# One shared expert in two parts around the private experts, and the third normalisation and router table inside the block of the weighted sum

## The reference

```python
xn = _layernorm(x, axis=-1)
x = x + _L0_gnn_ref(xn, edge_index, edge_weight, ...) + _L0_mix_ref(xn[None], ...)[0]
x = x + _L0_ffn_ref(_layernorm(x, axis=-1)[None], ...)[0]
xn = _layernorm(x, axis=-1)
x = x + _L1_gnn_ref(xn, edge_index, edge_attr_2, ...) + _L1_mix_ref(xn[None], ...)[0]
x = x + _L1_ffn_ref(_layernorm(x, axis=-1)[None], ...)[0]

def _L0_ffn_ref(x, Wr, W1s, b1s, W2s, b2s, W1p, b1p, W2p, b2p):
    shared = gelu(x @ W1s + b1s) @ W2s + b2s
    rw = jax.nn.softmax(x @ Wr, axis=-1)
    topw, topi = jax.lax.top_k(rw, K)
    ...
    return shared + routed

...
h = (x_flat @ W_gat).reshape(M, HEADS, NUM_EXPERTS)
a_src = (h * att_src).sum(-1)
a_dst = (h * att_dst).sum(-1)
```

## Time and profile before

| what | us |
|---|---|
| three runs, median (lowest to highest) | 3953.55 (3953.06 to 3957.26) |
| the profiled execution | 3953.38 |
| its span, first to last instruction | 3951.6 |
| busy: PE, DVE, ACT, POOL | 2606.2, 1907.8, 988.4, 2575.3 |
| mean granted clock of PE | 0.771 |

### The profile page before, as it was taken

The page is one execution under the profiler, slowest core; times in us unless marked ns, Lnnn a source line. Parts: engine busy times, 40 slices in busy tenths (PEclk is TensorE's granted clock), DMA queues, the critical chain, the costliest instruction groups (busy, mean ns, idle before and its releaser), DMA issues. The chain is left out here.

```text
span 3951.6 us, 42737 instructions
## 1 busy us (share of the span) xinstructions
PE 2606.2 (66%) x9484; PEld 1776.0 (45%) x9485; DVE 1907.8 (48%) x4550; ACT 988.4 (25%) x3007; POOL 2575.3 (65%) x4612
## 2 busy tenths in 40 slices
PE   0560004888875989999329666662357775697998
PEld 0350001333334778888325444442222223595776
DVE  8568822555553111111136688884257775553222
ACT  0120000000001212222012266552067775202111
POOL 0888886888878887777878888888278881000000
PEclk9975555565555999999769888886589996558999
DMA  1100004333341126666232222241011110000000
GB/s 47 33 17 19 8 2 148 104 105 105 104 83 56 35 74 193 197 194 194 82 93 56 50 51 50 50 48 6 3 10 8 8 8 2 0 0 27 11 11 33
DMA packets 179887, 229.35 MB, mean 58 GB/s; under 512 B 67275, under 2 KB 144445, under 8 KB 178749
## 3 DMA queue, kind: packets, MB, share of 16 engines
q0 software_dynamic: 81792, 103.39, 12.2%
q1 hardware_dynamic: 96828, 116.40, 9.3%
q10 hardware_dynamic: 1152, 8.39, 0.5%
HBM read 192.28 MB, written 35.73 MB: 58 GB/s over the span
## 5 line engine op out<-in xcount | busy, mean ns | idle before, releaser
L375 POOL DMA_INDIRECT slots_gnn<-rec_gnn,slot_row_gnn x782 | 775.9, 992 | 275.7 <-issue 153.7
L791 PE MATMUL banks<-rows_gnn,one_hot 128*128 128x256 f32 x832 | 459.2, 665 | 252.7 <-DMA rows_gnn<-support,slot_gnn 240.7
L1520 POOL DMA_INDIRECT arena<-table,slot_gnn x440 | 466.4, 1060 | 99.1 <-issue 88.9
L766 POOL DMA_INDIRECT rows_gnn<-support,slot_gnn x416 | 393.9, 947 | 96.4 <-issue 68.8
L791 PEld LDWEIGHTS banks<-rows_gnn,one_hot 128*128 128x128 f32 x832 | 198.9, 294 | 512.4 <-DMA rows_gnn<-support,slot_gnn 466.1
L766 POOL DMA_INDIRECT rows_router<-table_g,slot_router x304 | 310.6, 1022 | 130.8 <-POOLq L764 71.7
L1891 PE MATMUL banks<-score_diags,one_hot_m 128*128 128x512 f32 x608 | 291.9, 627 | 133.0 <-DVE group_max L1917 83.8
L1605 PE MATMUL banks<-weighted,one_hot 128*128 128x260 f32 x880 | 276.4, 470 | 73.6 <-ACT weighted L1581 72.9
L375 POOL DMA_INDIRECT slots_router<-rec_router,slot_row_router x256 | 260.4, 1017 | 72.4 <-issue 45.6
L1224 PE MATMUL banks<-xT,w 128*128 x960 | 267.7, 439 | 51.5 <-DMA w<-in_w2s 26.2
L469 PE MATMUL banks<-ident,xn 128*128 128x128 f32 x200 | 50.2, 396 | 349.2 <-DVE xn L450 349.2
(11 more groups left out here) (378 smaller groups left out, 4288.0 us busy)
## 6 DMA issues: line engine op xcount, KB each, us to landing
w_private<-in_w1p SPq DMA_DIRECT2D x32, 1024.0 KB
w_private<-in_w2p SPq DMA_DIRECT2D x32, 1024.0 KB
slots_gnn<-rec_gnn,slot_row_gnn POOLq DMA_INDIRECT x782, 2.1
slot_x<-zero_rows ACTq DMA_DIRECT2D x8, 1024.0 KB, 11.5
slot_rows<-slot_x SPq DMA_DIRECT2D x32, 256.0 KB
slot_y<-slot_out SPq DMA_DIRECT2D x32, 256.0 KB
arena<-table,slot_gnn POOLq DMA_INDIRECT x440
rows_gnn<-support,slot_gnn POOLq DMA_INDIRECT x416, 2.7
```

The costliest lines, as they stand in the source:

```text
L375: pool.indirect_dma_start(e.slots, bass.IndirectOffsetOnAxis(e.rows[:, j:j + 1], 0), e.rec[:, j, :], None)\
L766: pool.indirect_dma_start(e.rows_in[:, k, :], None, table, bass.IndirectOffsetOnAxis(row, 0))\
L791: pe.matmul(c.bank[:, k // per, 0:D], hot[:, k, :], e.rows_in[:, k, :], start=k % per == 0, stop=k % per == per - 1).then_inc(used, 1)
L1520: pool.indirect_dma_start(c.raw[:, t % RAW_RING, :], None, c.table1, bass.IndirectOffsetOnAxis(row, 0))\
```

## The change

Four things. First, the shared expert's weights are kept in a buffer of the whole block and loaded at its start (`load_shared0`), and its five chunks are done in two stages: three chunks before the private experts, two after them. In the second of these DVE also adds the fetched rows (`add_fetched0`), a few before each tile's own additions, up to a goal: 12 rows before tile 0 of its first chunk, two more with each tile, then 37 before the first tile of the second chunk, and the rest behind the last. Second, normalisation 3 and `table_g_stage` become stages of the sum's block, and Block C goes. Third, since more now lives in that block's memory, `AHEAD` is 120 for 128 and the ring 216 for 224 tiles. Fourth, the router's records are cut otherwise: 58, 40 and 158 for 58, 76, 34 and 88.

```diff
-EARLY = (58, 134, 168)
+EARLY = (58, 98)
+SHARED_FIRST = 3
...
+def load_shared0(c, block, weights):
+
+    w1, w2, b1, b2, biases, loaded = weights
+
+    @block.sync
+    def _(sp):
+        sp.dma_start(w1[:, 0, :, :], c.a["w1s"].rearrange("(k p) f -> p k f", p=P)).then_inc(loaded[0], 16)
+        sp.dma_start(w2[:, 0, :, :], c.a["w2s"].rearrange("(f p) d -> p f d", p=P)).then_inc(loaded[0], 16)
...
+        else:
+            for tile in range(nt):
+                beside(dve, tile, nt, y_done, tile + CHUNK_TILES)
+                add(0, tile, c.X[:, begin * CHUNK_TILES + tile, :], 1.0, tile % CHUNK_TILES)
+            beside(dve, nt, nt, y_done, nt + CHUNK_TILES)
...
+def add_fetched0(c):
+
+    state = [0]
+
+    def upto(dve, tile, tiles, y_done, done):
+        total = T * CHOSEN
+        t = tile % CHUNK_TILES
+        per_chunk = total // (tiles // CHUNK_TILES)
+        goal = total if tile == tiles else tile // CHUNK_TILES * per_chunk + per_chunk // 2 + 2 * t
+        dve.wait_ge(y_done, done)
+        while state[0] < goal:
...
-AHEAD = 128
-RAW_RING = 224
-ARENA = 224 * 2 * MSG
+AHEAD = 120
+RAW_RING = 216
+ARENA = RAW_RING * 2 * MSG
...
-                    scatter_records(c, block, s, eg, EARLY[0], EARLY[1])
                     fetch_outputs0(c, block, s)
+                    w_shared = expert_weights(c, s, "0", 1, FF0)
+
+                    load_shared0(c, block, w_shared)
...
-                                  lambda st, m: private_experts_stage(c, block, st, m)):
+                                  lambda st, m: shared(st, m, (0, SHARED_FIRST), None),
+                                  lambda st, m: private_experts_stage(c, block, st, m),
+                                  lambda st, m: shared(st, m, (SHARED_FIRST, CHUNKS), add_fetched0(c))):
...
-                        scatter_records(c, block, s, eg, EARLY[1], EARLY[2])
+                        scatter_records(c, block, s, eg, EARLY[0], EARLY[1])
                         gather_messages(c, block, s, e1, m + 2, m + 3)
-                        scatter_records(c, block, s, eg, EARLY[2])
+                        scatter_records(c, block, s, eg, EARLY[1])
...
-                        with ExitStack() as st:
-                            sum1_stage(c, block, st, e1)
+                        for stage in (lambda st, m: sum1_stage(c, block, st, e1, m),
+                                      lambda st, m: norm_stage(c, block, st, "3", m, False),
+                                      lambda st, m: table_g_stage(c, block, st, m)):
+                            m += 1
+                            with ExitStack() as st:
+                                stage(st, m)
...
-                    with nc.Block() as block:
-                        for stage in (lambda st, m: norm_stage(c, block, st, "3", m, False),
-                                      lambda st, m: table_g_stage(c, block, st, m)):
-                            m += 1
-                            with ExitStack() as st:
-                                stage(st, m)
-                    c.clear_spent()
```

More of the change, by code:

```diff
@@ new lines, in experts_stage @@
+def experts_stage(c, block, ctx, name, met_n, F, experts, b1_rows, b2_rows, gates, weights=None,
+                  chunks=None, beside=None):
+    E, FC = len(experts), F // P
+    begin, end = (0, CHUNKS) if chunks is None else chunks
+    nc_, nt = end - begin, (end - begin) * CHUNK_TILES
+    w1, w2, b1, b2, biases, loaded = expert_weights(c, ctx, name, E, F) if weights is None else weights
+    hid = c.sb(ctx, f"hidden_{name}_{begin}", [P, FC, 2, HALF_CHUNK])
+    part = c.sb(ctx, f"expert_out_{name}_{begin}", [P, 2, D])
+    h_ready = c.sem(ctx, f"hidden_ready_{name}_{begin}")
+    h_done = c.sem(ctx, f"hidden_gelu_{name}_{begin}")
+    y_ready = c.sem(ctx, f"out_ready_{name}_{begin}")
+    y_done = c.sem(ctx, f"out_added_{name}_{begin}")
+    biased = c.sem(ctx, f"out_biased_{name}_{begin}")
@@ L1205, in _ @@
     def _(sp):
[L1206 to L1212, removed]
+        if weights is None:
+            sp.dma_start(b1[:], b1_rows).then_inc(biases, 16)
+            sp.dma_start(b2[:].rearrange("p e d -> p (e d)"), b2_rows.partition_broadcast(P)).then_inc(biases, 16)
+            for e, (W1, W2) in enumerate(experts):
+                if e >= 2:
+                    sp.wait_ge(y_ready, (e - 1) * T)
+                sp.dma_start(w1[:, e % 2, :, :], W1.rearrange("(k p) f -> p k f", p=P)).then_inc(loaded[e % 2], 16)
+                sp.dma_start(w2[:, e % 2, :, :], W2.rearrange("(f p) d -> p f d", p=P)).then_inc(loaded[e % 2], 16)
         meet(sp, met, met_n)
@@ L1254, in _, with add @@
     def _(dve):
+        def add(e, tile, x, gate, t):
+            dve.wait_ge(y_ready, tile + (e * nt + 1))
+            dve.wait_ge(y_done, tile + (e * nt + CHUNK_TILES))
+            dve.tensor_tensor(part[:, 0, :], c.bank[:, 4 + t % 4, 0:D], b2[:, e, :], ALU.add)\
+                .then_inc(biased, 1)
+            dve.wait_ge(biased, tile + (e * nt + 1))
+            dve.scalar_tensor_tensor(x, part[:, 0, :], gate, x, ALU.mult, ALU.add).then_inc(y_done, 1)
         dve.wait_ge(biases, 32)
@@ L1269, in _ @@
-        meet(dve, met, met_n)
+        if beside is None:
+            for e in range(E):
+                with dve.Fori(0, nc_) as i:
+                    for t in range(CHUNK_TILES):
+                        tile = i * CHUNK_TILES + t
+                        at = i * CHUNK_TILES + (begin * CHUNK_TILES + t)
+                        x = c.X[:, ds(at, 1), :].rearrange("p a d -> p (a d)")
+                        gate = 1.0 if gates is None else gates[:, ds(at, 1), e:e + 1].rearrange("p a b -> p (a b)")
+                        add(e, tile, x, gate, t)
+        else:
[3 more added lines that the diff above has]
+            beside(dve, nt, nt, y_done, nt + CHUNK_TILES)
@@ L1549, in sum1_stage @@
     used = c.summed1
+    met = c.met
     per = GROUP // P
@@ L1588, in _ @@
         act.activation(rise[:], rise[:], ACT.Exp).then_inc(rise_exped, 1)
+        meet(act, met, met_n)
     @block.tensor
@@ L1624, in _ @@
         mm.then_inc(units, 1)
+        meet(pe, met, met_n)
     @block.vector
@@ L1767, in _ @@
         ch.then(dve.tensor_tensor(x, x, agg[:, :, 0:FEAT], ALU.add))
+        meet(dve, met, met_n)
+    @block.sync
+    def _(sp):
+        meet(sp, met, met_n)
 NE1 = 4
@@ L2271, in build @@
                     records.close()
+                    c.table_g = nc.dram_tensor("table_g", [NP, ROW_G], F32, kind="Internal").ap()
+                    c.tab = c.sb(l1, "tab_g", [P, T, ROW_G])
+                    c.edge_tab = c.sb(l1, "edge_tab", [P, T, 2 * NE1])
+                    c.high = c.sb(l1, "high", [P, T, NE1])
+                    c.lift = c.sb(l1, "lift", [P, 1])
                     with ExitStack() as s, nc.Block() as block:
```

84 lines of the change are left out of this document (33 added, 51 removed).

## The result

The changed kernel takes 3902.26 us (median of 4 runs, 3899.91 to 3902.39) and the kernel before 3953.31 (4 runs, 3952.53 to 3957.26): a ratio of 0.9867, 95% interval 0.985 to 0.9885. The profiled execution took 3902.39 us around a span of 3900.7, 51.0 less than before. The forecast was 3896, a gain of 57.0; the measured gain is 51.0, so it was 6 us smaller than worked out.

What follows compares the result with a forecast made beforehand. POOL's queue of indirect DMAs plus the hole before the router's gather was taken as the bound up to 2871 us. Hole -57.8 and last scatter +0.8 gave -57.0: 3953.4 to 3896 us, range 3884 to 3911.

Steps and rivals of the forecast that it cites:

- POOL's queue as the bound: From 1176 to 2871 us, POOL's indirect DMAs plus the hole before the router's gather were taken to set the time.
- The sum's shape: Shorter hole before the gather, -57.8 us, plus POOL's last scatter, +0.8, giving -57.0; the first block's 96 us bring nothing.
- that sign: POOL's last scatter was to lie within 5 us of 2799.7; moving by over 10 us would refute the prediction.
- Records beside the weights: Second graph's records before the fetch: 64 more meet private weights' traffic, 1.372 us each for 1.273; net +4.2 us.
- The end of the first block: Between the first block and the next: no term of its own; the second normalisation was expected near 1918.
- The wait at tile 120: POOL's messages: with AHEAD 120, POOL waits for the mix's end at 2232.4; +5.6 us of new wait.
- 70 more scatters: Router records behind the messages at the end of POOL's queue: 70 more at 1.27 us each, +88.9 us.
- The end of the second block: Between POOL's last scatter and the slot load before the router's gather: 11.3 us, low bound 6.1, 2 allowed upward.
- PE and the second part: Last two shared-expert chunks on PE, beside the fetch, 1837 to 1906; DVE ends at 1915.2 without holding POOL back.
- The rival of the lower clock: PE's second shared part falls to 1.2 GHz behind a meeting: +79 us, 3975 us, slower; chance 0.03.
- the cover: Moved normalisation and router table were to end at 2685 us, 115 us ahead of POOL's last scatter.
- The normalisation beside POOL: Third normalisation beside POOL's scatters costs one us; by the skill's two-port rule about 9 us, giving 3905 us.

Runs made afterwards that it cites:

- One part alone: Normalisation 3 and router table moved into the sum's block, shared expert whole, against the kernel before: 3899.7 us, ratio 0.9878.
- the other alone: Shared expert split, but normalisation 3 and router table in their own block, ring 224, AHEAD 128, against the kernel before: 3954.3 us, ratio 1.0016.
- twice the stage behind POOL's back: Changed kernel with normalisation 3 done twice in the sum's block: 3902.8 us, ratio 0.9879 to the kernel before.
- the first four runs: Four variants on one chip (stages moved only, shared expert split only, normalisation 3 doubled, two shared chunks early): 3899.7, 3954.3, 3902.8, 3916.9 us; kernel before 3948.4.
- two chunks first and the old goals: Changed kernel with two shared-expert chunks before the private experts and three behind, fetched-row goals unchanged: 3916.9 us, ratio 0.9919 to the kernel before.
- nine records moved: Kernel with only the stages moved, four router records more before the messages and five before tile 120: ratio 0.9991 to the kernel before, other chip.
- one memset shifted: Changed kernel with one more POOL memset before the fetch and one less behind the last router record: ratio 0.985 to the kernel before, other chip.

## Why the prediction was right, and by what it was off

**POOL's queue as the bound: right.** One part alone gives the gain, the other alone gives none, and twice the stage behind POOL's back costs nothing. The sum's shape held: the hole is gone, and of 92.8 us won in the first block nothing is left at POOL's last scatter. But that scatter moved by +9.9 us where +0.8 was forecast. It was to lie within 5 us of 2799.7 and came at 2808.80, so that sign failed, and it stayed only 0.1 short of the 10 us that the prediction named as refuting it. The sum missed by 5.5 us at the gather (-51.5 for -57.0), and only because a block end that came out 3.7 us shorter set off part of the 9.1; that is luck. The terms:

- **Records beside the weights, +4.2 forecast, +7.7 measured.** The rate was near right; 331 records fell beside the weights, 48 more than before, and the hitch among them is 6.13 us for 4.38. The scatters of the second graph's records, to be laid beside the earlier trace rows (stretch, its length, POOL's busy time and count, granted clock, DMA share, GB/s):

```profile
1316.40:1360.90 44.50, 32.82 (x35) 1.00 0.03 2
1360.90:1374.00 13.10, 9.29 (x10) 0.53 0.97 306
1374.00:1830.00 456.00, 316.87 (x331) 0.99 0.61 186
```

456.00 / 331 is 1.378 us for each, where I took 1.372; waits for own records to land are 32.7 us in all, 24.9 in the earlier trace rows. On the chip of the first four runs the split alone has 528.4 us for the 391 against 521.6 in the moved stages alone: +6.8, so the term is real and was mis-sized by some 3, about half of which can be the hitches: they come and go from one execution to the next.

- **The end of the first block, nothing forecast, +4.1 measured.** I had carried over the row at 2015.35 of the earlier trace rows, idle 6.60 before it, without a term of its own. It is 10.76 here. All kernels with the split shared expert have 10.75 to 10.77 (but 13.75 with two chunks first and the old goals, where DVE ended late), those without it 6.57 to 6.61.
- **The wait at tile 120, +5.6 forecast, 6.39 measured.** Right: the price of the smaller `AHEAD`, visible in the moved stages alone as well (7.19), and absent with `AHEAD` at 128. With the normalisation twice it is 2.56, while POOL there stood 5.45 us before the first message, for 2.62 here.
- **70 more scatters, +88.9, measured +89.9** (214.80 less 124.95).
- **The end of the second block, 11.3 forecast, 7.6 measured.** The slot load on SP starts 7.6 us after the last scatter, -3.7. My bounds of 6.1 and 13 held both ends; I took the nearest row of the same engine, and it was the wrong one. The moved stages alone have 11.4 (2805.70 to 2817.06), so the hole was nearly the forecast one there.

Beyond the forecast these are 3.5 + 4.1 + 0.8 + 1.0 - 3.7 = 5.7 us, for a miss of 5.5; the terms left out are below 0.7 each.

**PE and the second part: right.** It starts at 1835.94 (forecast 1837) and ends at 1908.75 (1906), and the clock stays up behind the meeting:

```profile
1874.10 17.39 PE L1242 MATMUL banks<-xT,w 128*128 x64
1891.32 17.43 PE L1252 MATMUL banks<-w,hidden 128*128 128x256 f32 x80
```

The rival of the lower clock did not come. DVE's last addition is at 1917.64, and 1915.2 was forecast. The next block, though, begins at 1925.42 (forecast near 1918), by the block's end above, and the third normalisation at 2640.87 (forecast 2626). The later normalisation costs nothing, since POOL too is 9 us later and the cover stays 118 us (115 forecast).

**The normalisation beside POOL, one us: right.** POOL's DMAs beside it take 0.95 to 1.13 us, and with the normalisation twice 0.84 us is all that comes on top. By the rule of the Trainium skill ("SBUF — State Buffer", Who interferes with whom), a VectorE operation in its two-port mode shuts GpSimd out, and some 9 us could have been lost there; this kernel's traces don't show the loss. That is no test of the rule: each of the 25 tensor_scalars takes 404 ns at the median, as long as a statistics operation over the same 256 values (408), and nothing in the traces tells that they ran in that mode.

**Not forecast:** what the split is for. With the stages moved and the shared expert whole, the router's table is stored at 2773.08 and POOL's last scatter is at 2805.70: 33 us of cover, the time between the two. With the split the cover is 118. The split moves slack from one side of POOL's queue to the other, and this kernel needs neither.

## What to carry to other kernels

Where one engine's queue runs through several blocks, sum its waits first: shortening a block for the other engines only moves that queue's entries, while work lifted out of a place where the queue stands is won in full, less what the memory for it costs (here 8 tiles of `AHEAD`, some 6 to 7 us: in the moved stages alone the hole is 57.0 us shorter and the gather 50.2 earlier). When additions from two sources are interleaved in one fixed order, ask for both what happens if it is late, as each can hold the other. And run the two halves of a change apart: one of them may be only slack, and may still be what pays on a slower chip.

## What the runs showed of the hardware that I had not expected

**A block's end has two prices on POOL.** From POOL's last memset to the next block's first instruction it is 5.9 us (before, first block), 10.0 (changed, first block), 10.2 (before, second block) and 6.5 (changed, second block). The barriers and the clearing of semaphores alone don't take that long: with two chunks first DVE ended last, and its next operation came 1.76 us later:

```profile
1947.90 2.38 DVE L414 BATCH_NORM_STATS2 stats<-x 128x6 f32<-128x256 f32 x7 [1.76 <-PEq L86]
```

The number of semaphores to clear, counted in the code, doesn't explain it (57 and 58 in the first block, where it grew; 58 and 72 in the second, where it shrank; in the split alone both blocks have 58 and take 10.0 and 6.5 us). Nor did shifts in POOL's list change it in the first block. The cause stays open; 4 us is what one should allow either way.

**Each of DVE's two long operations holds an indirect DMA.** As in the earlier trace rows, the two operations of 6.83 us above (each writes 128x6400 and reads two tensors in SBUF) coincide with two of POOL's of 7.16 and 6.55, and each of these ends 0.82 us after DVE's does. All six traces of this kind of chip have the pair, at 7.15 to 7.17 and 6.55 to 6.56:

```profile
2627.32 7.16 POOL L375 DMA_INDIRECT slots_router<-rec_router,slot_row_router  x1 [0.19 <-issue]
...
2634.79 6.55 POOL L375 DMA_INDIRECT slots_router<-rec_router,slot_row_router  x1 [0.19 <-issue]
```

**On other chips PE hardly gets on while POOL issues indirect DMAs.** Two kernels, the same stage in both (the whole shared expert, before the private ones). Columns: stretch, length, busy time and count of PE, its weight loads, DVE, ACT and POOL, granted clock, DMA share, GB/s. First the kernel before on the first chip:

```profile
1265.00:1437.00 172.00, 171.94 (x707) 135.66 (x708) 20.01 (x47) 36.89 (x44) 144.37 (x269) 0.99 0.11 33
```

Then the moved stages with nine records moved, on one of the others, up to POOL's last record and behind it:

```profile
1640.00:2355.00 715.00, 271.94 (x600) 152.74 (x600) 17.00 (x40) 31.09 (x37) 544.28 (x1019) 0.59 0.05 10
2355.00:2420.00 65.00, 49.72 (x199) 40.21 (x200) 6.48 (x14) 9.63 (x16) 0.29 (x2) 0.84 0.24 81
```

600 matmuls in 715 us beside POOL, 199 in 65 without it, against 707 in 172. Between them PE waits for nothing that the trace names:

```profile
1744.53 0.59 PE L1254 MATMUL banks<-w,hidden 128*128 128x256 f32 x1 [2.70 <-issue]
1745.93 0.58 PE L1254 MATMUL banks<-w,hidden 128*128 128x256 f32 x1 [0.82 <-issue]
```

(These two are of the kernel with one memset shifted.) And the tiny memset goes with a faster PE there. 500 us beside POOL's records of the second graph, in the kernel with one memset shifted, 414 matmuls (713 DMAs and memsets of POOL):

```profile
1705.00:2205.00 500.00, 175.16 (x414) 101.73 (x413) 15.00 (x34) 18.82 (x26) 380.80 (x713) 0.58 0.06 13
```

And 500 us of the same stretch in the kernel without memsets, 189 matmuls (372 DMAs):

```profile
1800.00:2300.00 500.00, 98.94 (x189) 54.11 (x189) 5.95 (x14) 7.63 (x9) 372.94 (x372) 0.53 0.03 2
```

What in POOL's issuing holds the others up on those chips, and why not on the first, no run here tells.
